# One chunk in every fifth edge group comes by SyncE's queue, row by row, instead of by GpSimd's gather

## The chip, the cores and the metric

The kernel runs on one core of a Trainium2 chip. The metric is device time in microseconds (us). Three runs of the kernel before took 3241.01, 3248.19 and 3255.64 us; their median, 3248.19 us, is its time.

## What is computed

One layer over a graph with 12,500 nodes (256 features) and 212,500 edges sorted by their end node. All is float32.

```python
xn = layernorm(x)
x = x + graph_attention(xn, edges) + mix(xn)      # 8 heads of 32; mix: linear attention and an MLP of 768
x = x + experts(layernorm(x))                     # top 2 of 8 experts, hidden 512
```

The graph attention is what matters here: for each edge and head a score `leaky_relu(s_src[src] + s_dst[dst])`, a softmax over the edges that end in one node, and the sum of `h[src]` weighted by it, with `h = xn @ W`.

## The kernel before, in words

**Stages.** A first stage (to about 150 us) computes for each node a row of 272 floats, its 256 features `h` and 2 x 8 scores, and stores it in DRAM as `table`. The edge stage (about 150 to 2330 us) goes over the edges. A last stage runs the experts.

**The edge stage.** The edges are cut into chunks of 128 (`P`) and groups of 16 chunks (`CB`); there are 104 groups and 1661 real chunks. `rows` has three buffers (`NR`), one per group in turn, each with 16 chunks of 128 rows of `table`, one row per edge on its own partition. For group k:
- GpSimd (`edges_pool`, line 1355) gathers the rows of each chunk with one indirect DMA, whose row numbers stand in `srcix` in SBUF. From group 3 on it waits before each gather until TensorE has summed that chunk of group k - 3 (semaphore `sum`), so that its place is free. Before group 102 it also gathers 16 tiles for the next stage (`first_fetches`, line 1342).
- ScalarE (`edges_scalar`, line 1474) copies the 16 scores of each row out (`copy_scores`, line 1478), once all of the group's gathers have landed (semaphore `rows_in`). TensorE transposes them, VectorE does the softmax within the group (`edge_scores`), TensorE transposes the weights back, VectorE multiplies the rows by them (`weigh`, line 1601 of the profile), TensorE sums each chunk by a matmul with a one-hot matrix (`sums`, line 1447), and ScalarE copies the sums to `fout` (line 1504) and stores them (lines 1530 and 1533).
- SyncE (`edges_sync`, line 1395) loads the edges' end and source ids for the break flags of group k + 2 (`edge_ids`, line 1386, its transfers on line 1392). It reads a flag that says whether the group has wide chunks (line 1406), and tells ScalarE on semaphore `far` that the buffer's stores are done (line 1416).

**What runs beside it.** The dense layers of `mix` are cut into steps that each engine runs between the parts of its groups. `Beside` (line 1309) is called four times per group on TensorE, VectorE, ScalarE and SyncE, and runs so many steps of its generators as a schedule has due at that call; the schedule is the same on all engines. SyncE's steps load and store what the MLP works on (`mlp_sync`, lines 1099, 1104 and 1116), each behind a wait for TensorE or VectorE. Calls 1 to 66 are about the attention part, up to call 360 (group 90) the MLP, then merges of the sums of nodes that lie in several chunks.

**Order.** Each engine's queue is in order, and so is what SyncE issues: a wait in front of a transfer holds back all that stands behind it.

**Row by row elsewhere.** Late in the kernel, `route_sync` (lines 2020 and 2021) has SyncE load a row number from SBUF into a register, check its bounds, and issue a transfer to that place, eight times in a row:

```python
at = sp.value_load(B.endrow[0:1, k:k + 1], min_val=k * REGION, max_val=(k + 1) * REGION - ET)
sp.dma_start(sorted_rows(B.sorted_d[bass.ds(at, ET), :]), B.pl_zero[:, :, :]).then_inc(S.e_z, 16)
```

The functions that the diff touches, with what calls them:

Of the kernel before, what the change touches and what calls it, by code (L numbers as in the profile page):

```python
# [7 lines left out]
F32 = mybir.dt.float32  # L8
# [6 lines left out]
P = 128  # L15
# [5 lines left out]
N_NODES = 12500  # L21
# [8 lines left out]
GH, GF = 8, 32  # L30
ROW = D + 2 * GH
CB = 16
# [19 lines left out]
SPLIT = 99  # L52
# [86 lines left out]
class Tally:  # L139


    def __init__(self, sem):
        self.sem, self.n = sem, 0
# [6 lines left out]
class Sems:  # L150
    def __init__(self, nc):
        new = nc.alloc_semaphore
        several = lambda name, n: [new(f"{name}{i}") for i in range(n)]
        self.stage = new("stage_done")
        self.const = new("constants")
        self.vec = new("vector_chain")

        self.ix_in, self.ix_rows, self.ix_fl = new("ix_in"), new("ix_ends_out_in"), new("ix_first_last")
        self.ix_tp, self.ix_cp, self.ix_num = new("ix_turned"), new("ix_copied"), new("ix_numbers")
        self.ix_hot, self.ix_hist, self.ix_sums = new("ix_hot_ready"), new("ix_histogram"), new("ix_sums")  # L160

        self.a_w, self.a_x, self.a_xt, self.a_h = new("a_weights_in"), several("a_x_in", NXB), several("a_xt_in", NXB), several("a_h_out", NXB)
        self.wcat, self.a_zero = new("wcat_ready"), new("frag_zeroed")
        self.xn, self.xnt, self.xt, self.h, self.hr, self.gram = (new(n) for n in (
            "norms_ready", "rows_turned", "xt_copied", "h_done", "h_copied", "gram_done"))
        self.gcopy = new("gram_copied")

        self.mix_in, self.mixp, self.mixv, self.mixa = new("mix_in"), new("mix_tensor"), new("mix_vector"), new("mix_scalar")

        self.es_in, self.es_sd, self.es_tp = new("ends_in"), new("ends_scores_copied"), new("ends_moved")  # L170

        self.rows_in, self.ds_in = several("rows_in", NR), several("ds_in", NR)
        self.near, self.far = several("near_out", 2), several("far_out", 2)
        (self.sce, self.tsc, self.flags, self.oh, self.inb, self.eav, self.fm, self.exp, self.tw, self.tail, self.wgh,
         self.sum, self.ev) = (new(n) for n in (
            "scores_copied", "scores_turned", "flags_ready", "onehot_ready", "scores_free", "edge_scores", "maxima_ready", "weights_exp",
            "weights_turned", "tails_ready", "rows_weighed", "chunk_summed", "chunk_copied"))

        self.m_w, self.m_xs, self.m_xt, self.m_o = new("m_weights_in"), new("m_x_in"), new("m_xt_in"), new("m_out")
        (self.m_pre, self.m_ready, self.m_q, self.m_x2, self.m_hn, self.m_tp, self.m_t, self.m_f1, self.m_g, self.m_f2, self.m_y,  # L180
         self.m_x3) = (new(n) for n in (
            "m_bias_sum", "m_weights_ready", "m_q_done", "m_x2_ready", "m_hn_ready", "m_hn_turned", "m_hnt_copied", "m_fc1_done",
            "m_gelu_done", "m_fc2_done", "m_y_added", "m_x3_ready"))

        self.mg_in, self.mg_out = new("mg_in"), new("mg_out")
        (self.mg_mt, self.mg_scan, self.mg_arg, self.mg_exp, self.mg_back, self.mg_lasts, self.mg_lt, self.mg_ax, self.mg_wd, self.mg_run,
         self.mg_rt, self.mg_pt, self.mg_sum) = (new(n) for n in (
            "mg_maxima_turned", "mg_scanned", "mg_exp_arguments", "mg_exp_done", "mg_turned_back", "mg_lasts_scaled", "mg_lasts_turned",
            "mg_alpha_spread", "mg_alpha_copied", "mg_run_done", "mg_run_turned", "mg_part_ready", "mg_summed"))

        self.e_w, self.e_x, self.e_x1 = new("e_gate_in"), several("e_x_in", NF), several("e_x1_out", NF)
        self.e_f, self.e_g = [several(f"e_frag_in{b}_", 2) for b in range(NF)], several("e_sorted_out", NH)
        self.e_const, self.e_zero, self.e_z = new("e_constants"), new("e_zero_ready"), new("e_pad_out")
        (self.e_rx1, self.e_mom, self.e_hn, self.e_tp, self.e_t, self.e_gate, self.e_got, self.e_max, self.e_exp, self.e_both, self.e_pos,
         self.e_carry, self.e_row) = (new(n) for n in (
            "e_x1_ready", "e_moments", "e_hn_ready", "e_hn_turned", "e_turns_copied", "e_gated", "e_logits_copied", "e_less_max", "e_exp_done",
            "e_both_ready", "e_positions", "e_carried", "e_rows_ready"))
        self.e_endrow, self.planned, self.e_pad = new("e_end_rows"), new("planned"), new("e_pad_rows_ready")
        self.free = new("early_free")

        self.x_w1, self.x_w, self.x_b = new("x_first_weights_in"), new("x_second_weights_in"), new("x_biases_in")
        self.x_in, self.x_y, self.x_wt = several("x_in", NI), several("x_out", NOUT), new("x_first_weights_copied")
        self.x_wc, self.x_bc = several("x_wc_in", NW), several("x_bc_in", NB)
        (self.x_tp, self.x_gt, self.x_f1, self.x_h, self.x_f2, self.x_st, self.x_aim) = (new(n) for n in (
            "x_turned", "x_in_copied", "x_fc1_done", "x_gelu_done", "x_fc2_done", "x_y_read_scaled", "x_aimed"))
# [114 lines left out]
class Bufs:  # L320


    def __init__(self, nc, a, out):
        self.a, self.out = a, out
        dram = lambda name, shape: nc.dram_tensor(name, shape, F32, kind="Internal").ap()
        self.table = dram("table", [N_PAD, ROW])
# [11 lines left out]
        self.nodeix = A("nodeix", [P, TILES], I32)  # L338
        keep = nc.sbuf_base
        self.gram = A("gram", [P, KD, D + 1], F32)  # L340
        self.wqa, self.bqa = A("wqa", [P, KD, D], F32), A("bqa", [P, D], F32)
        self.dfb, self.dlb, self.loc = A("dfb", [GH, CHUNKS], F32), A("dlb", [GH, CHUNKS], F32), A("loc", [P, CHUNKS], F32)
        self.srcix = A("srcix", [P, CHUNKS], I32)
# [182 lines left out]
def index_vector(v, vec, S, B):  # L526
# [39 lines left out]
    fragment_rows(v, vec, B.fr_node, B.nf, B.nid[:, :], B.nodeix, TILES)  # L566
    yield
    w = B.wide[:, :]
    v.wait_ge(S.ix_rows, 80)
    v.tensor_tensor(B.span[:, :], B.dlb[0:1, :], B.dfb[0:1, :], ALU.subtract).then_inc(S.ix_hot, 1)  # L570
    yield
    for i, cols in enumerate(SPANS):
# [201 lines left out]
def nodes_sync(sp, S, B):  # L774
# [25 lines left out]
    def heads(k):  # L800
        b, (s, n) = k % NXB, SUPERS[k]
        if k % 2 and k // 2 + NXB < len(X_PAIRS):
            load(k // 2 + NXB)
        sp.wait_ge(S.hr, tiles_to(k))
        sp.dma_start(rows_of(B.table, s, n), B.hr[b][:, 0:n, :]).then_inc(S.a_h[b], 16)
        if k in LOADED:
            load_turned(LOADED.index(k) + NXB)
        if k == ID_STEP:

            sp.wait_ge(S.ix_cp, len(TURNS) + 1)  # L810
            sp.dma_start(B.rows_d.rearrange("j (b c) -> (j b) c", c=P), B.flt[:, :]).then_inc(S.ix_rows, 16)
            sp.wait_ge(S.ix_rows, 16)
            for j, to in ((0, B.dfb), (1, B.dlb)):
                sp.dma_start(to[:, :], B.rows_d[j].partition_broadcast(GH)).then_inc(S.ix_rows, 16)
            for j, to, at in ((0, B.dfb_t, TAIL), (1, B.dlb_t, TAIL - 1)):
                sp.dma_start(to[:, :], B.rows_d[j, at:CHUNKS].partition_broadcast(GH)).then_inc(S.ix_rows, 16)

    for k in range(NS):
        heads(k)
# [532 lines left out]
            fetch_sums(p, S, B, r, i)  # L1352


def edges_pool(p, S, B, groups):
    for k in groups:
        b = k % NR
# [1 line left out]
            first_fetches(p, S, B)  # L1359
        for j in range(min(CB, REAL - k * CB)):  # L1360
            col = k * CB + j
            if k >= NR:
                p.wait_ge(S.sum, (k - NR) * CB + j + 1)
            p.indirect_dma_start(out=B.rows[b][:, j, :], out_offset=None, in_=B.table[:, :],  # L1364
# [30 lines left out]
def edges_sync(sp, S, B):  # L1395
    beside = Beside(mix_sync(sp, S, B), mlp_sync(sp, S, B), merge_sync(sp, S, B, WINDOWS[:-1]), first_sync(sp, S, B),
                    route_sync(sp, S, B, FIRST), first_weights(sp, S, B), merge_sync(sp, S, B, WINDOWS[-1:]))
    for k in range(GROUPS):
        if NR <= k + 2 < GROUPS:
            edge_ids(sp, S, B, k + 2)  # L1400
        for _ in range(3):
            beside()

        b = k % 2
        sums = 16 * CB * (k // 2)
# [9 lines left out]
        with sp.Else():  # L1415
            sp.sem_inc(S.far[b], 16 * CB)
        beside()
    beside.rest()


# [53 lines left out]
def edges_scalar(a, S, B):  # L1474
# [2 lines left out]

    def copy_scores(k):
        r, b = k % NR, k % 2
        a.wait_ge(S.rows_in[r], 16 * (CB * (k // NR) + min(CB, REAL - k * CB)))  # L1480
        a.wait_ge(S.tsc, max(k - 1, 0))
        a.activation(B.sc_e[b][:, :, :].rearrange("p j (c h) -> p j c h", h=GH),  # L1482
                     B.rows[r][:, :, D:ROW].rearrange("p c (j h) -> p j c h", h=GH), ACT.Copy).then_inc(S.sce, 1)
# [965 lines left out]
def experts_sync(sp, S, B):  # L2449
    def fetch(j):  # L2450
# [11 lines left out]
        ex = sp.value_load(B.expert[0:1, j:j + 1], min_val=0, max_val=EXPERTS - 1)  # L2462
        if j >= NW:
            sp.wait_ge(S.x_h, HT * (j - NW + 1))
        sp.wait_ge(S.x_b, 16)
        sp.dma_start(B.b1c[w][:, :], B.b1[:, bass.ds(ex, 1), :]).then_inc(S.x_wc[w], 16)
        if j >= NB:
            sp.wait_ge(S.x_st, 2 * (j - NB + 1))
# [203 lines left out]
def sync_program(sp, S, B):  # L2672
# [3 lines left out]
        edge_ids(sp, S, B, k)  # L2676
    edges_sync(sp, S, B)
    barrier(sp, S, 2)
    sp.dma_start(B.b1[:, :, :], B.a["L0_ffn_b1"].rearrange("e (k p) -> p e k", p=P)).then_inc(S.x_b, 16)
    late(route_sync(sp, S, B, LATER), experts_sync(sp, S, B))  # L2680
    for q in range(NF):
        sp.wait_ge(S.e_x1[q], max(stored_to(r) for r in range(q, len(ROUNDS), NF)))
# [40 lines left out]
```

## Time and profile before

| | |
|---|---|
| median of three runs | 3248.19 us (3241.01 to 3255.64) |
| the profiled execution's own time | 3240.78 us |
| its span, from the first to the last instruction | 3239.5 us |
| mean granted TensorE clock, share of full speed | 0.919 |
| busy share of the span: TensorE, VectorE, ScalarE, GpSimd | 82%, 62%, 48%, 69% |
| indirect gathers of GpSimd in the edge stage | 1661 of 128 rows |
| mean DMA rate | 173 GB/s |

The profile is of one execution. A row of a group has the line of the kernel, the engine, the operation, `out<-in` and a count; then the busy time and the mean time of one; then the idle time of the engine in front of it and what ended it. "issue" is time for which the profile shows no wait. An engine with a q behind its name (SPq, ACTq) is its queue: DMA issues, waits and register work, which are not counted as busy. PEld is TensorE's weight load, PE its matmul, DVE VectorE, ACT ScalarE, POOL GpSimd, SP SyncE.

### The profile page before, as it was taken

Reading aid. Unit: us, or ns where it says so; the run is one execution under the profiler, and the core shown is the slowest. Engines: PE = TensorE matmul, PEld = TensorE weight load, DVE = VectorE, ACT = ScalarE, POOL = GpSimd, SP = SyncE. Lnnn points to the kernel's source line nnn. Section 1 sums busy time; section 2 is a strip of 40 time slices with the busy share of each in tenths; the row PEclk is TensorE's granted clock in tenths of the full one; section 3 lists DMA queues with packets and bytes.
Section 4 is the critical chain, followed back from the end, with each engine's and each line's share of the span. In section 5 each row is a group of like instructions: output and inputs, shape, how many; then the busy total and the mean of one; then the engine's idle time right before and its main releaser. Section 6 shows DMA issues by size and latency. Waiting matters only on the chain.

```text
span 3239.5 us, 42164 instructions
## 1 busy us (share of the span) xinstructions
PE 2646.1 (82%) x11525; PEld 2052.0 (63%) x11525; DVE 2015.4 (62%) x5482; ACT 1553.4 (48%) x3392; POOL 2236.9 (69%) x2187
## 2 busy tenths in 40 slices
PE   7657776888898888988899886564578999999998
PEld 6546555666675666656566564442357887878887
DVE  7445567667676777767677676787554555445422
ACT  5325544555554556545465454343344545445444
POOL 0277777777777777777777777777557766776644
PEclk9879988999999999989999898887789999999999
DMA  8797766566566666666656666556666666666663
GB/s 274 245 297 210 198 176 171 162 173 179 164 172 178 175 178 169 166 179 173 178 164 170 178 163 175 161 156 191 217 177 160 155 156 160 151 143 127 139 109 61
DMA packets 397718, 561.17 MB, mean 173 GB/s; under 512 B 71976, under 2 KB 318030, under 8 KB 397305
## 3 DMA queue, kind: packets, MB, share of 16 engines
q0 software_dynamic: 123696, 298.61, 36.3%
q1 hardware_dynamic: 196457, 170.61, 18.0%
q10 hardware_dynamic: 77255, 88.59, 9.9%
q8 instruction: 99, 1.62, 0.2%
q14 instruction: 211, 1.73, 0.2%
HBM read 402.43 MB, written 169.68 MB: 177 GB/s over the span
## 4 chain that ended last, share of the span: by engine, by line
PE 65%; DMA 10%; ACT 9%; issue 6%; DVE 5%; POOL 5%; ACTq 1%; SPq 0%; DVEq 0%; POOLq 0%
PE bank L1447 21%; PE bank L2494 10%; PE bank L2507 9%; PE bank L1179 7%; DMA rows<-table,srcix 7%; PE bank L1168 5%; POOL rows L1364 4%; PE bank L1141 2%; PE bank L684 1%; PE bank L685 1%; PE bank L949 1%; ACT L1488 1%; DMA last_d<-fout 1%; ACT L1284 1%; ACT e_hn L2085 1%
## 5 line engine op out<-in xcount | busy, mean ns | idle before, releaser
L1364 POOL DMA_INDIRECT rows<-table,srcix x1536 | 1476.4, 961 | 468.1 <-issue 333.4
L1447 PE MATMUL bank<-rows,onehot 128*128 128x272 f32 x3328 | 921.6, 424 | 56.3 <-ACT fout L1504 51.9
L1504 ACT ACTIVATE fout<-bank 128x272 f32<-128x272 f32 x1659 | 638.6, 397 | 589.1 <-PE bank L1447 541.9
L1447 PEld LDWEIGHTS bank<-rows,onehot 128*128 128x128 f32 x3328 | 661.3, 206 | 239.7 <-ACT fout L1504 77.9
L1601 DVE TENSOR_TENSOR rows<-rows,bank 128x1024 f32<-128x1024 f32 x416 | 483.7, 1212 | 171.8 <-ACT rows L1493 171.3
L2585 POOL DMA_INDIRECT out<-x_y,x_dest x203 | 326.3, 1607 | 244.1 <-DMA out<-x_y,x_dest 157.3
L2494 PE MATMUL bank<-x_int,x_w1c 128*128 128x256 f32 (+1 forms) x1696 | 380.5, 378 | 23.0 <-issue 19.7
L2507 PE MATMUL bank<-e_w,x_ht 128*128 x1624 | 373.9, 383 | 8.4 <-issue 6.2
L2494 PEld LDWEIGHTS bank<-x_int,x_w1c 128*128 128x128 f32 x1696 | 317.5, 195 | 74.2 <-issue 32.2
L2533 ACT ACTIVATE x_ht<-bank,x_b1c 128x256 f32<-128x256 f32 (+1 forms) x424 | 172.9, 462 | 392.1 <-PE bank L2494 391.9
L2507 PEld LDWEIGHTS bank<-e_w,x_ht 128*128 128x128 f32 x1624 | 302.8, 192 | 51.3 <-issue 13.8
L1168 PE MATMUL bank<-m_hnt,fc_w 128*128 128x512 f32 (+1 forms) x600 | 289.9, 609 | 39.3 <-ACT m_hid L1284 30.5
L1179 PE MATMUL bank<-fc_w,m_hid 128*128 128x256 f32 x1176 | 270.2, 381 | 2.4 <-ACT m_hid L1284 2.4
L2562 DVE TENSOR_TENSOR x_y<-bank,x_b2c 128x512 f32<-128x512 f32 (+1 forms) x106 | 70.7, 667 | 321.2 <-PE bank L2507 321.2
L1574 DVE SCALAR_TENSOR_TENSOR g_sdm<-notself,bank 128x128 f32<-128x128 f32 x104 | 29.9, 287 | 364.5 <-PE bank L1430 363.9
L1429 PE MATMUL bank<-ident,sc_e 128*128 128x128 f32 x104 | 39.1, 376 | 260.8 <-ACT sc_e L1482 248.7
L1179 PEld LDWEIGHTS bank<-fc_w,m_hid 128*128 128x128 f32 x1176 | 224.5, 191 | 35.9 <-ACT m_hid L1284 2.8
L1947 POOL DMA_INDIRECT sorted_d<-e_hn,e_row x196 | 194.7, 993 | 65.4 <-issue 64.5
L1482 ACT ACTIVATE sc_e<-rows 128x256 f32<-128x256 f32 x104 | 43.3, 416 | 397.8 <-DMA rows<-table,srcix 349.4
L1566 DVE TENSOR_TENSOR onehot<-bank,loc 128x2032 f32<-128x2032 f32 x96 | 217.5, 2265 | 0.2
L1429 PEld LDWEIGHTS bank<-ident,sc_e 128*128 128x128 f32 x104 | 16.9, 162 | 302.1 <-ACT sc_e L1482 287.0
L1168 PEld LDWEIGHTS bank<-m_hnt,fc_w 128*128 128x128 f32 x600 | 120.5, 203 | 137.6 <-issue 77.1
(461 smaller groups left out, 3405.6 us busy)
## 6 DMA issues: line engine op xcount, KB each, us to landing
frag<-fout ACTq DMA_DIRECT2D x104, 544.0 KB
x_in<-sorted_d SPq DMA_DIRECT2D x97, 260.0 KB
rows<-table,srcix POOLq DMA_INDIRECT x1536
x_b2c<-in_L_ffn_b SPq DMA_DIRECT2D x106, 128.0 KB, 3.6
frag<-in_x ACTq DMA_DIRECT2D x1, 13416.0 KB
table<-hr SPq DMA_DIRECT2D x24, 544.0 KB, 4.0
xs<-in_x SPq DMA_DIRECT2D x24, 512.0 KB, 6.1
xg<-in_x SPq DMA_DIRECT2D x24, 512.0 KB, 6.0
```

Source lines behind the costliest of these rows:

```text
L1168: t = pe.matmul(bank[own[m % 2]][:, 0:n * P], B.mw1[:, kk, m * P:(m + 1) * P], B.m_hnt[:, kk, 0:n * P], start=(kk == 0), stop=(kk == KD - 1))
L1179: t = pe.matmul(bank[own[i // 2]][:, i % 2 * D:(i % 2 + 1) * D], B.m_hid[:, m, i * P:(i + 1) * P], B.mw2[:, m, :], start=(m == 0), stop=(m ...
L1364: p.indirect_dma_start(out=B.rows[b][:, j, :], out_offset=None, in_=B.table[:, :], in_offset=bass.IndirectOffsetOnAxis(ap=chunk_columns(B. ...
L1447: pe.matmul(B.banks[2 + c % 3][:, 0:ROW], B.onehot[k % 2][:, j, :], B.rows[k % NR][:, j, :], start=True, stop=True).then_inc(S.sum, 1)
L1504: a.activation(B.fout[k % 2][:, j, :], B.banks[2 + c % 3][:, 0:ROW], ACT.Copy).then_inc(S.ev, 1)
L1566: v.tensor_tensor(B.onehot[b][:, :, 0:P - 1], B.banks[0][:, 2 * P:3 * P - 1].unsqueeze(1).to_broadcast([P, CB, P - 1]), chunk_columns(B.lo ...
L1601: v.tensor_tensor(h, h, w.unsqueeze(3).to_broadcast([P, n, GH, GF]), ALU.mult).then_inc(S.wgh, 1)
L1947: p.indirect_dma_start(out=B.sorted_d[:, :], out_offset=bass.IndirectOffsetOnAxis(ap=B.e_row[:, j, at:at + 1], axis=0), in_=B.e_hn[r % NH] ...
L2494: t = pe.matmul(out, B.w1c[u][:, k, m * P:(m + 1) * P], B.gt[u][:, k, 0:n], start=(k == 0), stop=(k == KD - 1))
L2507: t = pe.matmul(bk[BANKS_OUT[u]][:, i * D:(i + 1) * D], B.ht[u][:, m, i * P:(i + 1) * P], B.w2[:, bass.ds(ex * HT + m, 1), :], start=(m == ...
L2533: a.activation(B.ht[u][:, m, 0:n], B.banks[BANKS_H[m * 2 // HT]][:, m % 2 * ET:m % 2 * ET + n], ACT.Gelu, bias=B.b1c[w][:, m:m + 1]).then_ ...
L2585: p.indirect_dma_start(out=B.out[:, :], out_offset=bass.IndirectOffsetOnAxis(ap=B.dest[j % (NOUT + 1)][:, i:i + 1], axis=0), in_=B.y[j % N ...
```

## The change

In groups 27, 32, ..., 97 (15 of them) GpSimd leaves out the last chunk. SyncE fetches its 128 rows with 128 transfers of one row into a spare buffer, which takes the place of an early matrix (`gram`) that is no longer used. It reads the 128 row numbers from the source ids in DRAM, 16 at a time, into registers. The work on one chunk is spread over 20 calls in five groups, 6 or 7 rows per call, and stands right behind SyncE's `beside` calls. At the last of these calls SyncE waits until all rows have landed and until TensorE has summed the chunk three groups earlier that has the place, and then copies the spare buffer there. ScalarE's `copy_scores` waits for one gather less on `rows_in` and, in these groups, for that copy too. The next chunk's rows start once the copy has landed. Two semaphores are new; to make room, two others are merged (`ix_rows` into `ix_in`, `x_b` into `e_w`), with the counts of their waits raised.

```diff
@@ Bufs
+        mark_gram, nc.sbuf_base = nc.sbuf_base, keep
+        self.spare = A("spare", [P, ROW], F32)
+        assert nc.sbuf_base <= mark_gram
+        nc.sbuf_base = mark_gram
...
+LOADS = 16
+SPARE_FROM, SPARE_EVERY = 20, 5
+SPARE_CALLS = 4 * SPARE_EVERY
+SPARE_GROUPS = list(range(SPARE_FROM + SPARE_EVERY + 2, SPLIT - 1, SPARE_EVERY))
+SPARE_CHUNK = CB - 1
+
+def spared_to(k, b):
+    return sum(g <= k and g % NR == b for g in SPARE_GROUPS)
+
+def spare_sync(sp, S, B):
+    sp.wait_ge(S.mixp, 5)
+    for i, g in enumerate(SPARE_GROUPS):
+        c, rows = g * CB + SPARE_CHUNK, [0] + [P * (t + 1) // SPARE_CALLS for t in range(SPARE_CALLS)]
+        if i:
+            sp.wait_ge(S.moved, 16 * i)
+        held_rows = {}
+        for lo, hi in zip(rows, rows[1:]):
+            for e in range(lo, hi):
+                if e % LOADS == 0:
+                    held_rows = dict(enumerate(B.nc.values_load_multi_w_load_instructions(
+                        B.src[c:c + 1, e:e + LOADS], engines=(mybir.EngineType.SP,), min_val=0, max_val=N_NODES)[1], e))
+                sp.dma_start(B.spare[e:e + 1, :], B.table[bass.ds(held_rows[e], 1), :]).then_inc(S.spare, 16)
+            if hi == P:
+                sp.wait_ge(S.spare, 16 * P * (i + 1))
+                sp.wait_ge(S.sum, (g - NR) * CB + SPARE_CHUNK + 1)
+                sp.dma_start(B.rows[g % NR][:, SPARE_CHUNK, :], B.spare[:, :]).then_inc(S.moved, 16)
+            yield
...
@@ edges_pool
+            if j == SPARE_CHUNK and k in SPARE_GROUPS:
+                continue
...
@@ edges_sync
+    spare = spare_sync(sp, S, B)
     for k in range(GROUPS):
         if NR <= k + 2 < GROUPS:
             edge_ids(sp, S, B, k + 2)
         for _ in range(3):
             beside()
+            if k > SPARE_FROM:
+                next(spare, None)
...
         beside()
+        if k > SPARE_FROM:
+            next(spare, None)
...
@@ copy_scores
-        a.wait_ge(S.rows_in[r], 16 * (CB * (k // NR) + min(CB, REAL - k * CB)))
+        a.wait_ge(S.rows_in[r], 16 * (CB * (k // NR) + min(CB, REAL - k * CB) - spared_to(k, r)))
+        if k in SPARE_GROUPS:
+            a.wait_ge(S.moved, 16 * (SPARE_GROUPS.index(k) + 1))
```

## Rows read from the trace of the kernel before

**Rows 1.** The page's chain that ended last, and its costliest group.
```profile
PE 65%; DMA 10%; ACT 9%; issue 6%; DVE 5%; POOL 5%; ACTq 1%; SPq 0%; DVEq 0%; POOLq 0%
...
L1364 POOL DMA_INDIRECT rows<-table,srcix x1536 | 1476.4, 961 | 468.1 <-issue 333.4
```

**Rows 2.** GpSimd in order of time, 1000 to 1013 us: start, length, idle before.
```profile
1000.90 0.95 POOL L1364 DMA_INDIRECT rows<-table,srcix  x1 [0.30 <-issue]
1002.16 0.95 POOL L1364 DMA_INDIRECT rows<-table,srcix  x1 [0.30 <-issue]
...
1008.49 0.95 POOL L1364 DMA_INDIRECT rows<-table,srcix  x1 [0.30 <-PE bank L1447]
1009.75 0.94 POOL L1364 DMA_INDIRECT rows<-table,srcix  x1 [0.30 <-PE bank L1447]
```

**Rows 3.** Line 1364 alone: ns min/median/max, and GpSimd's waits 595 to 2000 us.
```profile
L1364 POOL DMA_INDIRECT rows<-table,srcix x1536: 942/947/1717, 153.5 to 2096.6; - x192
L1364 POOL DMA_INDIRECT rows<-table,srcix_tail x125: 942/947/1937, 2098.0 to 2279.9; - x125
...
POOL rows L1364 <- issue: 239.6, 786, 0.3
POOL rows L1364 <- PE bank L1447: 98.7, 324, 0.3
```

**Rows 4.** Busy time in two stretches; then clock, DMA share, GB/s.
```profile
core 0: us, PE busy (x) PEld busy (x) DVE busy (x) ACT busy (x) POOL busy (x), PEclk, DMA share, GB/s
154.00:2281.00 2127.00, 1673.34 (x6706) 1230.81 (x6707) 1472.58 (x3302) 1039.23 (x2382) 1616.11 (x1677) 0.90 0.64 180
595.00:2000.00 1405.00, 1216.77 (x4817) 891.49 (x4816) 1006.53 (x2295) 738.69 (x1615) 1067.01 (x1110) 0.94 0.62 172
```

**Rows 5.** ScalarE's waits, 595 to 2000 us: us in total, times, longest.
```profile
ACT sc_e L1482 <- DMA rows<-table,srcix: 180.2, 48, 9.1
```

**Rows 6.** SyncE's waits, 595 to 2000 us.
```profile
SPq L1099 <- PE bank L1141: 634.7, 23, 37.8
SPq L1104 <- DVE m_x L1237: 500.4, 24, 38.3
SPq L1392 <- DVE notself L1560: 1.3, 3, 0.5
```

**Rows 7.** SyncE's lines 2020 and 2021, and their transfers in order of time.
```profile
L2020 SPq TENSOR_LOAD <-pl_endrow x8: 267/274/744, 3063.6 to 3072.1; - x8
L2020 SPq FUSED_REGOPS  x8: 152/152/152, 3063.9 to 3072.4; - x8
L2020 SPq SEQ_ASSERT  x8: 18/18/18, 3064.1 to 3072.6; - x8
...
L2021 SPq FUSED_REGOPS  x8: 37/37/37, 3064.2 to 3072.6; - x8
L2021 SPq MOVE sorted_d<-pl_zero x8: 29/29/29, 3064.3 to 3072.7; - x8
L2021 SPq DMA_DIRECT2D sorted_d<-pl_zero x8: 332/332/383, 3064.3 to 3072.8; - x8
...
3064.34 8.77 SPq L2021 DMA_DIRECT2D sorted_d<-pl_zero  x8
```

**Rows 8.** ScalarE's transfer of one descriptor, line 1533, and one of them.
```profile
L1533 ACTq DMA_DIRECT2D last_d<-fout x103: 232/363/577, 219.3 to 2317.7; - x103
...
1428.73 0.33 ACTq L1530 DMA_DIRECT2D frag<-fout  x1
1429.40 0.23 ACTq L1533 DMA_DIRECT2D last_d<-fout  x1
```

**Rows 9.** The loads of edge ids, line 1392, and their landing.
```profile
L1392 SPq DMA_DIRECT2D dsr<-in_src x104: 550/599/2406, 137.6 to 2243.4; - x104
...
DMA to landing us min/median/max: 2.3/5.0/19.9
```

More of the change, by code:

```diff
@@ L156, in __init__ @@
         self.vec = new("vector_chain")
-        self.ix_in, self.ix_rows, self.ix_fl = new("ix_in"), new("ix_ends_out_in"), new("ix_first_last")
+        self.ix_in, self.ix_fl = new("ix_ids_then_ends_in"), new("ix_first_last")
         self.ix_tp, self.ix_cp, self.ix_num = new("ix_turned"), new("ix_copied"), new("ix_numbers")
@@ L173, in __init__ @@
         self.near, self.far = several("near_out", 2), several("far_out", 2)
+        self.spare, self.moved = new("spare_in"), new("spare_moved")
         (self.sce, self.tsc, self.flags, self.oh, self.inb, self.eav, self.fm, self.exp, self.tw, self.tail, self.wgh,
@@ L189, in __init__ @@
             "mg_alpha_spread", "mg_alpha_copied", "mg_run_done", "mg_run_turned", "mg_part_ready", "mg_summed"))
-        self.e_w, self.e_x, self.e_x1 = new("e_gate_in"), several("e_x_in", NF), several("e_x1_out", NF)
+        self.e_w, self.e_x, self.e_x1 = new("e_gate_then_biases_in"), several("e_x_in", NF), several("e_x1_out", NF)
         self.e_f, self.e_g = [several(f"e_frag_in{b}_", 2) for b in range(NF)], several("e_sorted_out", NH)
@@ L199, in __init__ @@
         self.free = new("early_free")
-        self.x_w1, self.x_w, self.x_b = new("x_first_weights_in"), new("x_second_weights_in"), new("x_biases_in")
+        self.x_w1, self.x_w = new("x_first_weights_in"), new("x_second_weights_in")
         self.x_in, self.x_y, self.x_wt = several("x_in", NI), several("x_out", NOUT), new("x_first_weights_copied")
@@ L323, in __init__ @@
     def __init__(self, nc, a, out):
+        self.nc = nc
         self.a, self.out = a, out
@@ L568, in index_vector @@
     w = B.wide[:, :]
-    v.wait_ge(S.ix_rows, 80)
+    v.wait_ge(S.ix_in, 112)
     v.tensor_tensor(B.span[:, :], B.dlb[0:1, :], B.dfb[0:1, :], ALU.subtract).then_inc(S.ix_hot, 1)
@@ L810, in heads @@
             sp.wait_ge(S.ix_cp, len(TURNS) + 1)
-            sp.dma_start(B.rows_d.rearrange("j (b c) -> (j b) c", c=P), B.flt[:, :]).then_inc(S.ix_rows, 16)
-            sp.wait_ge(S.ix_rows, 16)
+            sp.dma_start(B.rows_d.rearrange("j (b c) -> (j b) c", c=P), B.flt[:, :]).then_inc(S.ix_in, 16)
+            sp.wait_ge(S.ix_in, 48)
             for j, to in ((0, B.dfb), (1, B.dlb)):
-                sp.dma_start(to[:, :], B.rows_d[j].partition_broadcast(GH)).then_inc(S.ix_rows, 16)
+                sp.dma_start(to[:, :], B.rows_d[j].partition_broadcast(GH)).then_inc(S.ix_in, 16)
             for j, to, at in ((0, B.dfb_t, TAIL), (1, B.dlb_t, TAIL - 1)):
-                sp.dma_start(to[:, :], B.rows_d[j, at:CHUNKS].partition_broadcast(GH)).then_inc(S.ix_rows, 16)
+                sp.dma_start(to[:, :], B.rows_d[j, at:CHUNKS].partition_broadcast(GH)).then_inc(S.ix_in, 16)
     for k in range(NS):
@@ L2464, in fetch @@
             sp.wait_ge(S.x_h, HT * (j - NW + 1))
-        sp.wait_ge(S.x_b, 16)
+        sp.wait_ge(S.e_w, 48)
         sp.dma_start(B.b1c[w][:, :], B.b1[:, bass.ds(ex, 1), :]).then_inc(S.x_wc[w], 16)
@@ L2678, in sync_program @@
     barrier(sp, S, 2)
-    sp.dma_start(B.b1[:, :, :], B.a["L0_ffn_b1"].rearrange("e (k p) -> p e k", p=P)).then_inc(S.x_b, 16)
+    sp.dma_start(B.b1[:, :, :], B.a["L0_ffn_b1"].rearrange("e (k p) -> p e k", p=P)).then_inc(S.e_w, 16)
     late(route_sync(sp, S, B, LATER), experts_sync(sp, S, B))
```

## Prediction

> **What bounds the kernel now.** I read the page first, then GpSimd's queue, then what the other engines wait for, then SyncE's queue. On the page the longest group is GpSimd's gather of table rows, 1536 times 0.96 us, and the chain that ended last runs through the group sums, the landing of gathered rows and the gather itself [rows 1]: it does not name one engine. GpSimd's own order of time does. Gather follows gather: 0.95 us of work, 0.30 us until the next one starts, whatever is written as the releaser [rows 2]. No wait of a gather for a sum of TensorE is longer than that same 0.3 us, and the rest is put down to issue [rows 3], so the wait for a free buffer costs nothing. From the first gather at 153.5 us to the last at 2279.9 us [rows 3] GpSimd makes 1677, 16 of them for the next stage [rows 4]: one every 2126.4 / 1676 = 1.27 us, and 0.947 + 0.30 = 1.25 us where nothing lengthens one [rows 2, 3]. A group of 16 takes 20.0 us. The others have room: over 1405 us of this stage TensorE is busy 87%, VectorE 72%, ScalarE 53% [rows 4], and ScalarE still waits 180 us in 48 places for gathered rows to land [rows 5]. So in this stage GpSimd's queue sets the pace, and **a gather taken off it is worth 1.25 us**, as long as nothing else becomes slower than GpSimd.
>
> **What the change removes.** One gather in each of 15 groups (27, 32, ..., 97), with its wait for the buffer: 15 x 1.25 = 18.8 us. The bytes are the same, they only come by another queue.
>
> **What it adds to SyncE.** For a moved chunk SyncE issues 128 transfers of one row (1088 bytes), 8 loads of 16 row numbers from DRAM into registers, a bounds check of each number, a wait for the last row, a wait for the buffer and one transfer from the spare buffer. This is spread over 20 places in five groups. What stands behind it in SyncE's queue is all that the stage asks of SyncE: the edge ids that VectorE's break flags need two groups later, the sign to ScalarE that a result buffer is free, the loads and stores of the dense layers beside it, and then the sign that the moved chunk is there, for which ScalarE's copy of the scores now waits (TensorE's transpose, in front of the next group's sums, waits for that copy). If SyncE takes longer than GpSimd for five groups, all of these come late and SyncE sets the pace.
>
> *What SyncE has to give.* With the change GpSimd needs 79 x 1.25 = 98.8 us for five groups. SyncE waited 634.7 + 500.4 + 1.3 = 1136.4 of the 1405 us [rows 6]; the other 269 us are 70 groups' own work, 3.8 us each, 19.2 us in five. That leaves 79.6 us, or **0.62 us a row with everything**.
>
> *What a row costs.* The nearest rows are eight rounds late in the kernel, in which SyncE loads one number, checks it, computes an address and issues a transfer [rows 7]: load 0.274, check 0.152 and 0.018, address 0.037 and 0.029, transfer 0.332, together 0.842 us. Eight issues take 8.77 us from the first start to the last end, so a round is (8.77 - 0.33) / 7 = 1.206 us, and at most 0.06 us lies in each of six gaps; some loads were longer than their median, and I take 0.045.
> - Transfer: those above feed 128 partitions. One of a single descriptor, ScalarE's store of the last rows, took 0.363 us right behind another transfer and 0.232 us where it started 0.34 us after the end of the one before [rows 8]. A row's transfer has register work in front of it, so it is nearer to the second: I take 0.25, bounds 0.23 and 0.36. With address and three gaps 0.037 + 0.029 + 0.135 + 0.25 = 0.45 us (0.43 to 0.56).
> - Check: 0.152 + 0.018 and two gaps are 0.26 us. The 0.152 stands right behind a load and may hold a wait for it; an operation on registers of the same kind takes 0.037. Behind one load of 16 numbers most checks should be of the second kind: 0.16 us (0.15 to 0.26).
> - Loads: a load of one number from SBUF takes 0.274 us [rows 7]. One of 16 from DRAM costs between that (0.3 with its gap) and sixteen such loads, 5.0 us. Nearest is a trip to the same array: the shortest time in which the ids came in from DRAM, 2.3 us [rows 9]. Eight times that is 18.4 us (2.5 to 40).
> - Ends: the last row has to land before the move; 3 us (0 to 6), since the move's own landing lies beside other work.
>
> The sum is 128 x (0.45 + 0.16) = 78.1, 18.4 and 3: 99.5 us, and with SyncE's own 19.2 us **118.7 us for five groups**, against 100.0 us (80 x 1.25) before. SyncE would be the bound, 18.7 us longer in each of 15 windows, 280 us; about one group (20 us) is its lead, since ids are asked for two groups ahead. That leaves +260 us, with GpSimd's gain used up. The profiled execution took 3240.8 us, so 3501; it lies 7.4 us under the median of the runs shown (3248.2), and on that scale I say 3508 us. The low ends give 128 x 0.58 + 2.5 + 19.2 = 95.9 us, which fits under 98.8; the high ends 128 x 0.82 + 40 + 6 + 19.2 = 170 us, +1030 us.
>
> Only a page has a price for the load of registers from DRAM. The Trainium skill (Runtime: NRT & Kernel Launch, Instruction fetch mechanics) gives about 200 ns per register, also in bulk, which no row of this trace shows; by that, as an estimate, a load of 16 is 3.2 us and the time some 110 us above mine.
>
> *Priced at nothing.* The merged semaphores: each wait counts landings that are long in by then. The transfers themselves: DMA engines are busy 62% here [rows 4] and the bytes were moved before too; a copy inside SBUF of 139 KB per five groups is added. GpSimd's skip has no instruction.
>
> On the use of a second queue the trace and a rule differ. The gaps of 0.30 us behind every gather show that issue on GpSimd, not the bytes, sets the pace [rows 2]. The Trainium skill (DMA: Bandwidth & Descriptors, Issuing engines are not separate DMA queues) says that starting DMAs on several engines saves only sequencer time, usually small beside the DMA. By that rule the 18.8 us would not be there and the time would stay at 3248 us; the trace speaks against that. The same page (Rules for kernel authors) advises to gather many small transfers into one, which speaks against 128 single rows; rows 7 and 8 agree, as a small transfer costs a queue about what a large one does.
>
> **Rivals.**
> 1. *SyncE keeps up.* If checks and loads are near their low ends, its 96 us and little more stay under GpSimd's 98.8 and GpSimd sets the pace, 18.8 us shorter: 3229 us, 0.6% faster. For it: SyncE sits idle 81% of this stage now [rows 6]. Against: it needs nearly every price at its low end. The point that decides is 0.62 us a row.
> 2. *SyncE keeps up on average, but the moved chunk comes late.* The last rows go out in the last step before ScalarE needs them; landing (2.3 us or more), the move's issue and its landing make some 8 us in which TensorE stands still once in five groups. ScalarE's spare 180 us over 70 groups [rows 5], 2.6 a group, can make up 13 us in five, so it costs between nothing and about the gain: 3232 to 3248 us, no change that can be told.
> 3. *Each number is loaded by itself.* Then a row costs about a whole round of rows 7, 1.09 to 1.21 us: 128 x 1.1 + 3 + 19.2 = 163 us, 63 us more a window, over 4100 us.
>
> **How the numbers follow.** SyncE over its budget, my forecast, has 0.58, of which 0.08 is rival 3 or near it. Rival 1 has 0.27, rival 2 0.15. A measurement of this kernel can tell about 0.5% (16 us) from no change. Rival 1's 18.8 us lie just over that, so a little of it counts as no change: faster 0.24, same 0.18, slower 0.58. Predicted 3508 us. The forecast's own range is 3280 to 3720 us; the other sign holds much of the chance, so the range that is to hold 8 in 10 starts at 3226 us.
>
> **What would show it.** Right: in groups 21 to 97 SyncE has hardly a wait left for TensorE or VectorE, GpSimd's gathers show waits for sums well over 0.3 us, a group takes about 23.7 us, and ScalarE's score copy waits for SyncE or for the move. The steps: the transfer of a row near 0.25 us, the check near 0.06 us busy, the load near 2.3 us. Wrong: gathers still 1.25 us apart with SyncE still waiting; then the time falls by 15 gathers. If group 97 ends on time but the rest is late, the cause lies elsewhere than in SyncE's queue.

## The result and the profile after

The kernel with the change takes **3762.79 us** (median of 4 runs, 3748.67 to 3769.24); the kernel before, with a fourth run, 3244.6 us. The ratio is **1.1596, 95% interval 1.1564 to 1.1628**: 16% slower, 518 us. The forecast named slower as the likeliest side and SyncE as the bound, but 3508 us is 255 us short, and 3762.79 lies above the range's 3720.

From the page of the kernel with the change: the span, the chain that ended last (by engine, then the first four lines of it), and GpSimd's gather and ScalarE's score copy among the costliest groups.
```profile
span 3759.7 us, 52139 instructions
...
SPq 40%; PE 30%; issue 16%; DMA 4%; DVE 4%; ACT 4%; POOL 2%; ACTq 0%; DVEq 0%; POOLq 0%
SPq L1385 19%; SPq L1387 17%; PE bank L2543 9%; PE bank L2556 8%; PE bank L1494 5%; POOL rows L1406 2%; SPq L1434 2%; DMA rows<-table,srcix 2%; SPq L1451 2%; PE bank L690 1%; PE bank L691 1%; PE bank L955 1%; ACT e_hn L2134 1%; PE bank L2532 1%; ACT xg L932 1%
...
L1406 POOL DMA_INDIRECT rows<-table,srcix x1522 | 1459.7, 959 | 972.6 <-PE bank L1494 657.4
...
L1531 ACT ACTIVATE sc_e<-rows 128x256 f32<-128x256 f32 x104 | 43.3, 416 | 730.4 <-DMA rows<-spare 521.8
```
SyncE's queue had 0% of the chain [rows 1]; now it has 40%, nearly all of it on two lines: 1385, which loads and checks row numbers, and 1387, which computes an address and issues one row's transfer. A gather itself is as long as before (959 ns against 961), but GpSimd's idle time has doubled, from 468 to 973 us, and most of it now ends with TensorE's sums (line 1494, the line 1447 of before). ScalarE's score copy waits 522 us, 15 times, for the transfer out of the spare buffer.

The stretch in which SyncE fetches rows, 595 to 2500 us: first the busy times with TensorE's clock, DMA share and rate, then the waits of SyncE's and of GpSimd's queue (us in total, times, longest).
```profile
595.00:2500.00 1905.00, 1267.42 (x4856) 924.57 (x4856) 1022.59 (x2316) 750.08 (x1643) 1085.45 (x1132) 0.84 0.48 131
```
```profile
SPq L1110 <- DVE m_x L1243: 19.1, 1, 19.1
SPq L1391 <- DMA spare<-table: 12.4, 13, 1.1
SPq L1385 <- DMA rows<-spare: 2.5, 12, 0.3
SPq L1105 <- PE bank L1147: 0.5, 1, 0.5
...
POOL rows L1406 <- PE bank L1494: 590.5, 380, 38.0
POOL rows L1406 <- issue: 229.3, 752, 0.5
```
SyncE waited 1136 of 1405 us [rows 6]; now 35 of 1905. GpSimd, whose gathers never waited more than 0.3 us for a sum [rows 3], waits 590 us, 38.0 us at the longest. About the same number of instructions (4856 matmuls against 4817 [rows 4]) takes 1905 us in place of 1405. That is 36% longer, and the other engines do about as much work in it as before, so all of them were kept waiting. TensorE's mean granted clock fell from 0.94 to 0.84 of full speed, but TensorE is busy 67% of the stretch now against 87%, so it is not what holds the others up.

The time is lost where the new work stands. Between ScalarE's score copies of groups 22 and 97 lie 15 windows of five groups: 101.6 us each before, 137.1 with the change, 15 x 35.5 = 532 us more. From group 97's copy to the last group's it takes 146.9 us instead of 164.0: GpSimd, whose rows lay waiting for SyncE's, has 77 gathers of table rows left by then and not 91 (14 x 1.25 = 17.5 us), while TensorE runs 361 matmuls in that stretch in both kernels. 532 - 17 = 515, and the spans differ by 520.2.

SyncE's lines 1385, 1387 and 1391 by themselves (instruction, count, ns min/median/max, first and last start):
```profile
L1385 SPq FUSED_REGOPS  x1920: 147/147/175, 601.7 to 2666.9; - x192
L1385 SPq SEQ_ASSERT  x1920: 18/18/18, 601.9 to 2667.1; - x192
L1385 SPq TENSOR_LOAD <-in_src_ptr x120: 990/1158/2848, 597.3 to 2659.5; - x120
L1385 SPq ALU_OP  x120: 41/50/62, 599.5 to 2661.1; - x120
L1385 SPq TENSOR_LOAD <-in_src x120: 1840/2013/3845, 599.6 to 2661.2; - x120
...
L1387 SPq FUSED_REGOPS  x1920: 37/37/52, 605.7 to 2674.7; - x192
L1387 SPq MOVE spare<-table x1920: 29/29/42, 605.8 to 2674.8; - x192
L1387 SPq DMA_DIRECT2D spare<-table x1920: 217/225/1872, 605.9 to 2674.8; - x192
...
L1391 SPq DMA_DIRECT2D rows<-spare x15: 538/553/564, 754.1 to 2676.2; - x15
DMA to landing us min/median/max: 2.0/2.0/2.1
```
One load of 16 numbers covers 16 rows (120 loads, 1920 rows), each in two steps: the array's address (`in_src_ptr`), then the numbers. Then come 16 checks in a row, and the rows' transfers, partly in later calls. The next table sets every SyncE instruction between group 22's and group 97's score copy, its duration and the gap in front of it, against the terms of the forecast's sum.

| in five groups, us | forecast | measured | how |
|---|---|---|---|
| 128 transfers with their addresses | 57.6 | 58.0 | 37.6 transfers, 11.1 address, 9.3 move of a register |
| 128 checks | 20.5 | 32.8 | 24.7 compare, 8.1 assert |
| 8 loads | 18.4 | 27.5 | 16.6 numbers, 10.2 address of the array, 0.7 arithmetic |
| what SyncE did before | 19.2 | 16.3 | the rest, the move out of the spare buffer with it |
| waits | 3 | 2.5 | what is left of 137.1 |
| sum | 118.7 | 137.1 | |

### The profile page after: what moved, and what is told of

It is laid out like the page before. It is cut to its first block, busy times and chain, and to the rows that moved or that the text cites. A ratio compares the mean times of both kernels' runs of the same rounds, so it can differ in the third digit from the quotient of the medians.

```text
span 3759.7 us, 52139 instructions
## 1 busy us (share of the span) xinstructions
PE 2683.1 (71%) x11525; PEld 2075.3 (55%) x11525; DVE 2019.5 (54%) x5482; ACT 1552.3 (41%) x3392; POOL 2214.9 (59%) x2172
## 4 chain that ended last, share of the span: by engine, by line
SPq 40%; PE 30%; issue 16%; DMA 4%; DVE 4%; ACT 4%; POOL 2%; ACTq 0%; DVEq 0%; POOLq 0%
SPq L1385 19%; SPq L1387 17%; PE bank L2543 9%; PE bank L2556 8%; PE bank L1494 5%; POOL rows L1406 2%; SPq L1434 2%; DMA rows<-table,srcix 2%; SPq L1451 2%; PE bank L690 1%; PE bank L691 1%; PE bank L955 1%; ACT e_hn L2134 1%; PE bank L2532 1%; ACT xg L932 1%
## 5 line engine op out<-in xcount | busy, mean ns | idle before, releaser
L1406 POOL DMA_INDIRECT rows<-table,srcix x1522 | 1459.7, 959 | 972.6 <-PE bank L1494 657.4
L1494 PE MATMUL bank<-rows,onehot 128*128 128x272 f32 x3328 | 938.3, 429 | 72.3 <-ACT fout L1553 65.3
L1494 PEld LDWEIGHTS bank<-rows,onehot 128*128 128x128 f32 x3328 | 669.7, 209 | 260.9 <-ACT fout L1553 92.6
L2543 PE MATMUL bank<-x_int,x_w1c 128*128 128x256 f32 (+1 forms) x1696 | 382.0, 380 | 23.1 <-issue 19.2
L1174 PE MATMUL bank<-m_hnt,fc_w 128*128 128x512 f32 (+1 forms) x600 | 283.6, 598 | 11.9 <-ACT m_hid L1290 11.1
L1185 PE MATMUL bank<-fc_w,m_hid 128*128 128x256 f32 x1176 | 279.1, 390 | 2.4 <-ACT m_hid L1290 2.4
L1185 PEld LDWEIGHTS bank<-fc_w,m_hid 128*128 128x128 f32 x1176 | 232.1, 197 | 39.9 <-ACT m_hid L1290 2.8
```

The costliest lines, as they stand in the source:

```text
L1174: t = pe.matmul(bank[own[m % 2]][:, 0:n * P], B.mw1[:, kk, m * P:(m + 1) * P], B.m_hnt[:, kk, 0:n * P], start=(kk == 0), stop=(kk == KD - 1))
L1185: t = pe.matmul(bank[own[i // 2]][:, i % 2 * D:(i % 2 + 1) * D], B.m_hid[:, m, i * P:(i + 1) * P], B.mw2[:, m, :], start=(m == 0), stop=(m ...
L1494: pe.matmul(B.banks[2 + c % 3][:, 0:ROW], B.onehot[k % 2][:, j, :], B.rows[k % NR][:, j, :], start=True, stop=True).then_inc(S.sum, 1)
L2543: t = pe.matmul(out, B.w1c[u][:, k, m * P:(m + 1) * P], B.gt[u][:, k, 0:n], start=(k == 0), stop=(k == KD - 1))
```

## Experiments

Two theories stood: that SyncE's own instructions are the bound, with checks and loads dearer than forecast; and the forecast's second rival, that ScalarE's wait for the moved chunk stops the chain. Each edit is against the kernel with the change unless it says otherwise. Run beside the first four, the kernel before took 3244 us; beside the last four, 3240.5.

### Without the bounds check

```diff
-                        B.src[c:c + 1, e:e + LOADS], engines=(mybir.EngineType.SP,), min_val=0, max_val=N_NODES)[1], e))
+                        B.src[c:c + 1, e:e + LOADS], engines=(mybir.EngineType.SP,), min_val=0, max_val=N_NODES,
+                        skip_runtime_bounds_check_because="the ids are node numbers, 0 to N_NODES")[1], e))
```

> SyncE fetches as in the change, but the row numbers' bounds are not checked at run time (1920 checks less). Theory A, SyncE's queue sets the pace by its own work: in the changed kernel's trace a check takes about 0.252 us from start to start, so 128 of them are 32.3 us of a five-group window of 137 us; without them 105 us, still just over GpSimd's 98.8, so 3763 - 15 x 32.3 = about 3280 us, and SyncE has still hardly any wait. Theory B, the moved chunk arrives late (last row's landing, wait, move and its landing follow each other in front of ScalarE's score copy, whatever SyncE did before): checks don't matter much, over 3650 us.

Measured: 3348.08 us, ratio 1.0314 (1.0272 to 1.0355), slower than was expected. GpSimd's waits for sums, 595 to 2000 us:
```profile
POOL rows L1407 <- PE bank L1495: 195.3, 315, 10.6
```
Without two instructions per row, 0.165 us by their medians, 415 of the 518 us are gone. (That is not the checks' share of the loss. The loss is what SyncE's whole work has over GpSimd's pace, and without the transfers of rows, in the last experiment, all 518 are gone.) A window is 109.5 us, 27.6 less; the 32.8 us of checks are not all got back. By the same sum as in the table the transfers of rows rise from 37.6 to 40.3 us and the waits from 2.5 to 4.4.

### Row numbers from SBUF

```diff
-        self.spare = A("spare", [P, ROW], F32)
+        self.spare, self.spare_ids = A("spare", [P, ROW], F32), A("spare_ids", [len(SPARE_GROUPS), P], I32)
...
+    first = SPARE_GROUPS[0] * CB + SPARE_CHUNK
+    sp.dma_start(B.spare_ids[:, :], bass.AP(B.src.tensor, first * P, [[SPARE_EVERY * CB * P, len(SPARE_GROUPS)], [1, P]])).then_inc(S.spare, 16)
+    sp.wait_ge(S.spare, 16)
...
-                        B.src[c:c + 1, e:e + LOADS], engines=(mybir.EngineType.SP,), min_val=0, max_val=N_NODES)[1], e))
+                        B.spare_ids[i:i + 1, e:e + LOADS], engines=(mybir.EngineType.SP,), min_val=0, max_val=N_NODES)[1], e))
...
-                sp.wait_ge(S.spare, 16 * P * (i + 1))
+                sp.wait_ge(S.spare, 16 * P * (i + 1) + 16)
```

> The row numbers of all 15 chunks are loaded into SBUF once, and SyncE reads them from there, 16 at a time, with the checks left in. Theory A: a load of 16 from DRAM costs 3.1 us now (a pointer 1.1 us, the numbers 1.9 us); from SBUF about 0.3 to 0.6 us, so 8 x 2.6 = 21 us less per window, 116 us, and about 3450 us. Theory B: over 3650 us. If each number from SBUF costs 0.27 us by itself, a load of 16 takes over 4 us and the time goes up instead, to some 3880 us.

Measured: 3560.44 us, ratio 1.096 (1.0918 to 1.1003). The load and the check of this kernel:
```profile
L1388 SPq FUSED_REGOPS  x1920: 147/147/169, 603.6 to 2470.9; - x192
...
L1388 SPq TENSOR_LOAD <-spare_ids x120: 984/1258/4062, 602.4 to 2465.8; - x120
```
The load of the address is gone, and the 16 numbers take 1.26 us instead of 2.01. It saves 202 us, less than expected: a load of 16 registers is slow from SBUF too, nearly five times the 0.274 us that one number took [rows 7]. The check is 147 ns here as well, so its length has nothing to do with where the numbers come from.

### Both together

Against the kernel with row numbers from SBUF:

```diff
-                        B.spare_ids[i:i + 1, e:e + LOADS], engines=(mybir.EngineType.SP,), min_val=0, max_val=N_NODES)[1], e))
+                        B.spare_ids[i:i + 1, e:e + LOADS], engines=(mybir.EngineType.SP,), min_val=0, max_val=N_NODES,
+                        skip_runtime_bounds_check_because="the ids are node numbers, 0 to N_NODES")[1], e))
```

> Both: row numbers from SBUF and no checks. Theory A: SyncE's work per window falls from 137 to about 84 us, under GpSimd's 98.8 us; GpSimd sets the pace again with 15 gathers less: 3245 - 19 = about 3226 us, and SyncE waits for TensorE and VectorE again. Theory B: over 3600 us. Between them: if the late arrival costs what ScalarE can make up only in part, 3235 to 3260 us.

Measured: **3225.51 us** (12 runs), ratio **0.9936 (0.9916 to 0.9957)**. This one is faster than the kernel before by 18.5 us, where either edit alone was slower. Its waits between 595 and 2000 us, SyncE's, GpSimd's, and those of ScalarE's score copy:
```profile
SPq L1110 <- DVE m_x L1243: 69.1, 17, 22.6
SPq L1105 <- PE bank L1147: 48.8, 13, 9.8
SPq L1395 <- DMA spare<-table: 27.2, 13, 3.5
SPq L1388 <- DMA rows<-spare: 11.2, 13, 2.9
...
POOL rows L1410 <- issue: 232.5, 763, 0.3
POOL rows L1410 <- PE bank L1498: 106.6, 350, 0.3
...
ACT sc_e L1535 <- DMA rows<-spare: 106.3, 12, 13.2
```
SyncE waits again for the engines that it serves, and no gather waits more than 0.3 us: GpSimd sets the pace, as before. The two edits save 415 and 202 us alone, 617 in all, but 537 together, since nothing is gained below GpSimd's pace. The row on ScalarE matters too: the moved chunk does come late (its move is issued 0.9 to 14.0 us after the group's last gather has ended), ScalarE waits for it 12 times, 13.2 us at the longest, and still no gather is held up.

### Only left out

GpSimd leaves the 15 chunks out, and nobody fetches them; they are computed from what their places held before.

```diff
-    spare = spare_sync(sp, S, B)
+    spare = iter(())
...
-        if k in SPARE_GROUPS:
-            a.wait_ge(S.moved, 16 * (SPARE_GROUPS.index(k) + 1))
```

> GpSimd leaves out the last chunk of the 15 groups and nobody fetches it (those chunks are computed from what an earlier group left in the buffer), so the run shows what GpSimd's 15 gathers are worth by themselves. If GpSimd's queue sets the pace alone: 15 x 1.25 = 18.8 us less than the kernel before, about 3226 us. If another engine is as slow as GpSimd, less: 3235 to 3245 us.

Measured: 3223.6 us, ratio 0.9924 (0.9897 to 0.9952). GpSimd's gathers alone are worth some 20 us, the 15 x 1.25 = 18.8 of the forecast within the interval. No way of fetching these 15 chunks can be expected to take less than leaving them out, and the kernel with both edits stands 2 us above it, less than the intervals can tell, with SyncE's 1920 transfers, loads, waits and moves in it. So what the transfers load on the DMA engines costs nothing that can be told either; it can't be where the 518 us came from.

### Only SyncE's part

SyncE fetches the rows into the spare buffer and does nothing with them; GpSimd gathers every chunk and ScalarE waits as before.

```diff
-        if i:
-            sp.wait_ge(S.moved, 16 * i)
...
-                sp.wait_ge(S.sum, (g - NR) * CB + SPARE_CHUNK + 1)
-                sp.dma_start(B.rows[g % NR][:, SPARE_CHUNK, :], B.spare[:, :]).then_inc(S.moved, 16)
...
-            if j == SPARE_CHUNK and k in SPARE_GROUPS:
-                continue
...
-        a.wait_ge(S.rows_in[r], 16 * (CB * (k // NR) + min(CB, REAL - k * CB) - spared_to(k, r)))
-        if k in SPARE_GROUPS:
-            a.wait_ge(S.moved, 16 * (SPARE_GROUPS.index(k) + 1))
+        a.wait_ge(S.rows_in[r], 16 * (CB * (k // NR) + min(CB, REAL - k * CB)))
```

> SyncE fetches all 15 chunks row by row as in the change, with DRAM loads and checks, but into the spare buffer only: GpSimd gathers every chunk as before, nothing is moved and ScalarE waits for nothing more. Theory A, SyncE's work by itself sets the pace, through the ids, signs and loads that stand behind it: about 134 us per window against 137 us, 3763 - 15 x 3 = about 3720 us, and VectorE and TensorE wait for SyncE's loads. Theory B, what is slow is ScalarE's wait for the moved chunk: without that wait about the time before, 3245 us.

Measured: 3770.88 us (2 runs), ratio 1.1625 (1.1584 to 1.1665): as slow as the whole change, with no move and nobody waiting for one. VectorE's waits for SyncE's transfers, 595 to 2500 us, first in the kernel with the change:
```profile
DVE neq L1606 <- DMA dsr<-in_src: 246.1, 36, 11.6
...
DVE m_x L1209 <- DMA xm_d<-m_x: 157.8, 16, 24.4
```
and in this one:
```profile
DVE neq L1598 <- DMA dsr<-in_src: 489.3, 58, 19.4
...
DVE m_x L1209 <- DMA xm_d<-m_x: 282.3, 22, 23.8
```
The same loss shows at another place: where ScalarE's wait for the move was, VectorE now waits nearly twice as long for the edge ids and for the dense layers' data, which stand behind the rows in SyncE's queue. The wait for the move is where the loss was seen, not where it came from.

### Every tenth group

7 chunks, the rest as in the change, checks and loads included.

```diff
-SPARE_FROM, SPARE_EVERY = 20, 5
+SPARE_FROM, SPARE_EVERY = 20, 10
```

> The change as it was, checks and DRAM loads included, but for one chunk in every tenth group (7 chunks, 40 calls each). Theory A: SyncE's work per ten groups is about 112 us for the chunk and 40 us of its own, 152 us, under GpSimd's 198.8: GpSimd sets the pace with 7 gathers less, 3244 - 8.8 = about 3235 us, no change that can be told. Theory B, a stop per moved chunk: 7 stops of 35 us, about 3480 us.

Measured: 3236.86 us (10 runs), ratio 0.9989 (0.9965 to 1.0013): no difference. SyncE's waits of 595 to 2000 us in this kernel:
```profile
SPq L1105 <- PE bank L1147: 192.1, 22, 30.6
SPq L1110 <- DVE m_x L1243: 113.3, 23, 20.6
```
The same instructions, at half the density, cost nothing that can be told: SyncE has 157.8 us of work in ten groups that take 200.7. So the 518 us are no price per instruction; they are what goes over GpSimd's pace. Seven gathers would be worth 7 x 1.25 = 8.8 us, which this interval (-11 to +4 us) holds but doesn't show.

### Every fourth group

18 chunks, against the kernel with both edits.

```diff
-SPARE_FROM, SPARE_EVERY = 20, 5
+SPARE_FROM, SPARE_EVERY = 20, 4
```

> Like the run with row numbers from SBUF and no checks, but for one chunk in every fourth group (18 chunks). Theory A: that run's SyncE waited about 10% of its time, so a chunk costs it some 67 us and its own work 4.4 us a group; in four groups 84.6 us against GpSimd's 63 x 1.25 = 78.8, so SyncE is the bound again, by 4.6 us over the 80 us before in each of 18 windows, less its lead: about 3244 + 65 = 3310 us. If that run's gain grows with the number of chunks (18 x 1.25 = 22.5 us): 3222 us.

Measured: 3397.82 us, ratio 1.0461 (1.0422 to 1.0501), well over what was expected. GpSimd's waits for sums, then SyncE's, 680 to 2200 us (from the first full window on):
```profile
POOL rows L1410 <- PE bank L1498: 271.7, 369, 13.1
...
SPq L1395 <- DMA spare<-table: 20.5, 17, 2.8
SPq L1105 <- PE bank L1147: 20.5, 7, 8.1
SPq L1110 <- DVE m_x L1243: 10.8, 7, 2.4
```
In four groups SyncE has 85.1 us of work by the same sum, where GpSimd needs 63 x 1.25 = 78.8. A window took 89.5 us, against 81.3 for four groups before: 18 x 8.2 = 148 of the 157 us. The 4 us or so between 85.1 and 89.5 are waits that stay although SyncE is behind, for the last row's landing and for steps of the dense layers that TensorE and VectorE have not done. What SyncE had waited in the kernel with both edits was not all slack.

### Loads and checks without transfers

The kernel of "Only SyncE's part" without the transfer of a row and the wait for it.

> SyncE loads the row numbers from DRAM and checks them as in the change, but issues no row transfers; GpSimd gathers everything as before. Theory A: loads and checks are 57 us of a window, with SyncE's own work about 80 us, under 100 us: the time before, 3245 us, since neither part alone is too much. If the DRAM loads or the checks delay SyncE's other work by their length alone, over 3300 us.

Measured: 3241.08 us, ratio 0.9989 (0.9969 to 1.001). GpSimd's waits for sums, 595 to 2000 us:
```profile
POOL rows L1397 <- PE bank L1485: 102.4, 336, 0.3
```
SyncE's work in five groups is 80.3 us here, under the 100 that GpSimd needs for 80 gathers, and it is hidden. Loads and checks are no burden by themselves. The change fails on their sum with the transfers.

## Why the prediction was right, and where it failed

**Right.** *The bound and the point that decides*: GpSimd's queue set the pace before (15 gathers are worth 20.4 us by "Only left out", 18.8 by the forecast), and SyncE's does with the change. The budget of 0.62 us a row holds in both directions. By the table a row costs (58.0 + 32.8 + 27.5) / 128 = 0.92 us with everything, and the kernel is slow. With both edits the same sum is 72.0 / 128 = 0.56 us, and it is GpSimd's pace again, 18.5 us faster. For every fourth group SyncE's other work is 13.0 us of the 85.1, the budget (78.8 - 13.0) / 128 = 0.51, and there 0.56 us a row was too slow. *The transfer with its address*: 58.0 us against 57.6, from one pair of ScalarE's transfers [rows 8]. *What shows it*: SyncE without waits, gathers that wait for sums, ScalarE and VectorE waiting for what SyncE issues. A group took 27.4 us, though, not 23.7.

**Right by luck.** The lead came to 17 us against 20, but not by the forecast's way. It was to come from ids that are asked for two groups ahead, so at the start, but the first of the 15 windows took 134.5 us already. What came back came at the end, from the 14 gathers that GpSimd was ahead. In "Only SyncE's part", where ScalarE waits for no move, the first window took 102.8 us: there SyncE's lead does show. With the move, ScalarE's copy starts about 2.1 us after the move is issued, in all 15 groups: it waits for the last of SyncE's work, and the ids' two groups of lead don't help.

**The step that failed** is the price of checks and loads. *Check*: 0.16 us was taken, on the thought that the 0.152 us of [rows 7] held a wait for the load in front, and that a check behind a load of 16 would cost the 0.037 us of another register operation. All 1920 took at least 147 ns, fifteen of sixteen of them with no load right in front. The check was worth the 0.26 us of the high end: 32.8 us, 12.3 over the forecast. *Loads*: a landing of edge ids, 2.3 us [rows 9], was a fair stand-in for the numbers (2.09 us with the gap), but a load from DRAM is two loads here, and the one of the array's address (1.29 us) was in no term. 27.5 us, 9.1 over. The remaining terms differ by -3.0 together, so a window is 18.4 us longer than forecast: 276 us in 15. A window of before was 101.6 us and not 100.0, which takes 24 us back, and the lead gave 3 less. 276 - 24 + 3 = 255 us, of the 258 by which the rise of 518 us exceeds the forecast's 260.

The range failed with it. The prediction gives no working for its upper end, 3720 us; all the high ends together were 1030 us over the kernel before. The check stood at its high end and the load two fifths of the way to its own.

**Rival 1**, that SyncE keeps up, is false for the change and true for it with both edits: 3225.51 us, 3229 forecast. **Rival 2**, that the moved chunk comes late, happens in that kernel, and costs about the 2 us between it and "Only left out", if anything: ScalarE's spare time takes it up, as the lower of its two ends had it. **Rival 3**, each number by itself, is false: 120 loads for 1920 rows.

**The two rules.** "Only left out" and "Both together" show that GpSimd's part in starting 15 gathers was worth about 20 us in this stage, and that another queue can take it over at no cost that can be told. The Trainium skill (DMA: Bandwidth & Descriptors, Issuing engines are not separate DMA queues) grants just that, the sequencer's time, and calls it usually small; here it is the bound, and the rule would have left the time where it was.

The loads of 16 registers took 2.01 us from DRAM and 1.26 from SBUF, by their medians. The Trainium skill (Runtime: NRT & Kernel Launch, Instruction fetch mechanics) gives about 200 ns per register; the runs give 126 and 79 ns. The time that it led to, 110 us above the forecast, was nearer all the same, because the load of the address made up for the difference.

## What to carry to other kernels

Before work is moved to an idle queue, compare the sum of its instructions there, gaps included, with the pace of the bounding engine over the same stretch: under it the work cost nothing here that can be told, and over it nearly every further microsecond was paid, so two instructions of together 0.165 us, 1920 times, decided 415 us of time. Where such a queue is short of time, bring the row numbers into SBUF first and leave out the run-time check where the data can't break it. Idle time of a queue is not all spare: a part of it is waiting for others that a fuller queue can't use.

## What was not expected of the hardware

- A compare for a bounds check took SyncE 147 ns, the same kind of register instruction for an address 37 ns, wherever either stood. With the assert and the gaps a check came to (24.7 + 8.1) / 128 = 0.26 us, about as much as issuing a transfer.
- A load of 16 registers took 1.26 us from SBUF against 0.274 for one [rows 7]. From DRAM it took 2.01 us, and 1.16 more for the array's address.
- A transfer of one row took SyncE 0.225 us by the median and 0.217 at the least, but up to 1.87 us; with its gap the mean was 0.295, and it rose to between 0.31 and 0.34 in the kernels of the experiments that were faster. What the transfers wait for in the slow cases was not tested.
